# Fourier attention on one core: ScalarE's rounding moved between cosine and sine, and the query projections, output projection, residuals and norms moved to other places within the chunks

## The reference

```python
def _fourier_kernel(x, proj_mat):
    p = jnp.einsum('blhd,dm->blhm', x, proj_mat) / math.sqrt(D_HEAD)
    return jnp.concatenate([jnp.cos(p), jnp.sin(p)], axis=-1) / math.sqrt(D_KMAP)
...
x2 = _layer_norm(x, ln1_g, ln1_b)
q = (x2 @ wq + bq).reshape(B, L, N_HEAD, D_HEAD)
k = (x2 @ wk + bk).reshape(B, L, N_HEAD, D_HEAD)
v = (x2 @ wv + bv).reshape(B, L, N_HEAD, D_HEAD)
qp = _fourier_kernel(q, proj_mat)
kp = _fourier_kernel(k, proj_mat)
kv = jnp.einsum('blhm,blhd->bhmd', kp, v)
attn = jnp.einsum('blhm,bhmd->blhd', qp, kv)
attn = attn.reshape(B, L, D_MODEL) @ wo + bo
x = x + attn
```

## Time and profile before

| | us |
|---|---|
| device time, three runs | 891.72, 892.42, 892.43 (median 892.42) |
| device time of the profiled execution | 885.71 |
| its span, first to last instruction | 883.9 |
| busy in the span: PE, DVE, ACT, POOL | 731.3, 686.8, 570.6, 394.5 |
| mean granted TensorE clock | 0.903 of full speed |
| K0 to Q3, from the first cosine of K0 to the copy of the last output | 225.4 |

### The profile page before, as it was taken

How to read it: one execution, slowest core, us unless ns; L and a number is a source line. 1 busy time by engine, 2 the same in 40 slices (tenths; PEclk the granted TensorE clock), 3 DMA queues, 4 the chain that set the end, 5 groups by cost and what they waited for, 6 DMA issues and landing times. The chain is left out here.

```text
span 883.9 us, 11015 instructions
## 1 busy us (share of the span) xinstructions
PE 731.3 (83%) x3306; PEld 469.4 (53%) x3306; DVE 686.8 (78%) x1615; ACT 570.6 (65%) x926; POOL 394.5 (45%) x427
## 2 busy tenths in 40 slices
PE   4788998779998889999778988877778767877787
PEld 3666765445555567777566867643223222222565
DVE  6685786798998638777767888968899778786785
ACT  5264664657474435664636767667899879777776
POOL 6638665634345105555329977534323332230330
PEclk9999998988697669999969999987899889789999
DMA  4200000100000000000001000000000000000001
GB/s 134 72 12 13 16 16 18 34 24 25 13 25 19 0 1 1 1 1 0 1 0 37 1 1 0 1 0 1 1 0 1 1 1 0 1 0 1 1 1 48
DMA packets 9610, 11.59 MB, mean 13 GB/s; under 512 B 720, under 2 KB 5712, under 8 KB 9552
## 3 DMA queue, kind: packets, MB, share of 16 engines
q1 hardware_dynamic: 9552, 10.89, 4.3%
HBM read 9.84 MB, written 1.05 MB: 12 GB/s over the span
## 5 line engine op out<-in xcount | busy, mean ns | idle before, releaser
L1032 POOL TENSOR_TENSOR rbuf<-B,rbuf 128x512 fp32r<-128x512 f32 x96 | 124.1, 1295 | 83.6 <-ACT rbuf L960 83.4
L497 POOL TENSOR_SCALAR small<-small 128x4 f32<-128x4 f32 x32 | 8.5, 265 | 173.3 <-DVE small L387 172.8
L994 DVE TENSOR_TENSOR B<-B,up_banks 128x512 f32<-128x512 f32 x68 | 46.4, 683 | 42.3 <-PE up_banks L733 25.8
L945 ACT ACTIVATE B<-gate_banks 128x512 f32<-128x512 f32 x68 | 40.6, 599 | 59.4 <-PE gate_banks L733 58.3
L960 ACT ACTIVATE rbuf<-B 128x512 fp32r<-128x512 f32 x100 | 62.5, 625 | 17.3 <-DVE B L1010 12.3
L1010 DVE TENSOR_TENSOR B<-B,spread_bank 128x512 f32<-128x512 f32 x96 | 64.7, 678 | 11.0 <-ACT B L949 7.0
L1757 ACT ACTIVATE B<-B,VEC 128x1024 f32<-128x1024 f32 x48 | 55.3, 1151 | 22.4 <-DVE B L1752 22.3
L731 PE MATMUL gate_banks<-XH,WH 128*128 128x512 f32 x152 | 67.0, 441 | 0.8 <-ACT YT L1355 0.8
L733 PE MATMUL gate_banks<-XH,WL 128*128 128x512 f32 x152 | 62.4, 410 | 0.0
L732 PE MATMUL gate_banks<-XL,WH 128*128 128x512 f32 x152 | 62.3, 410 | 0.0
L949 ACT ACTIVATE B<-gate_banks,WR 128x512 f32<-128x512 f32 x64 | 44.0, 689 | 27.3 <-PE gate_banks L733 26.7
(11 more groups left out here) (347 smaller groups left out, 2274.3 us busy)
## 6 DMA issues: line engine op xcount, KB each, us to landing
STG<-in_w_split SPq DMA_DIRECT2D x27, 256.0 KB, 2.7
X<-in_x SPq DMA_DIRECT2D x4, 256.0 KB, 5.0
out<-X SPq DMA_DIRECT2D x4, 256.0 KB, 2.3
WR<-in_w_raw SPq DMA_DIRECT2D x1, 524.5 KB, 4.4
STG<-in_w_exact SPq DMA_DIRECT2D x2, 256.0 KB, 2.6
STG<-in_w_split SPq DMA_DIRECT2D x5, 64.0 KB, 1.9
STG<-in_w_split SPq DMA_DIRECT2D x1, 192.0 KB, 2.4
STG<-in_w_split SPq DMA_DIRECT2D x1, 128.0 KB, 2.0
```

What stands on the lines that cost most here:

```text
L994: nc.vector.tensor_tensor(MO[n % 2], AO[n % 2], U[n % 2][:, :], ALU.mult).then_inc(mul_done, 1)
L1032: e_.tensor_tensor(lo, hidden(f, n), hi.bitcast(F32), ALU.subtract).then_inc(hl_ready, 1)
```

## The change

In both halves of the stage ScalarE's order within a slot becomes cosine of p, projection copy, round of p+2, sine of p; it was cosine, sine, round, (output or YT copy,) projection copy. The rounds of pairs 19 and 27 (slot 3 of K2 and K3) go from ScalarE to VectorE. The projections of Q1 to Q3 begin two slots earlier (TensorE in slots 0 to 3, copies and splits in 1 to 4). The split of the attention output goes from VectorE (slot 2) to GpSimd (slot 1, ahead of the first projection split); the product with wo goes from slot 1 to slot 4 and waits for the last projection copy, its copy YT from slot 2 to slot 5. In the query bodies the tail goes on TensorE from slot 3 (1 in Q0) to 5 and on VectorE from slot 4 (2 in Q0) to 7; norm steps go to slots 1, 3 and 6 on VectorE, 2 and 3 on GpSimd, 4 on TensorE and 5 on ScalarE. KVT is filled in slot 2 of Q0 and not in slot 1. In FFN2's table two steps trade places by two blocks (2 from 7 to 9, 8 from 9 to 8, 9 from 11 to 10, 3 from 8 to 11).

```diff
-            16: {..., 5: (6,), 7: (2, 7), 8: (3,), 9: (8,), 11: (9,), 14: (10,)},
+            16: {..., 5: (6,), 7: (7,), 8: (8,), 9: (2,), 10: (9,), 11: (3,), 14: (10,)},
...
-            if cp > NC + 1 and s_ == 0:
-                pe.wait_ge(yt_ready, count(6, cp - NC - 2) + 1)
+            if cp > NC + 2 and s_ == 0:
+                pe.wait_ge(yt_ready, count(6, cp - NC - 3) + 1)
...
         def rounds_on_act(p):
-            return p % 2 == 1
+            return p % 2 == 1 and not (p // UP in (2, 3) and p % UP == 3)
...
-            s_ = n - (1 if cp <= NC else 2)
+            s_ = n - (1 if cp <= NC else 0)
...
         def lin_pool(g, cp, hook):
             for n in range(UP):
+                if n == 1 and cp > NC:
+                    project_pool(g, cp - NC - 1)
                 if lin_projects(cp + 1, n - 1) is not None:
                     lin_split(nc.gpsimd, g, cp + 1, lin_projects(cp + 1, n - 1))
-                lin_hooks(n, hook, 1, {0: (0,), 1: (1,)})
+                lin_hooks(n, hook, 1, {0: (0,), 1: (1,)} if cp < NC else {2: (0,), 3: (1,)})
...
         lin_pe
-                if n == 1 and cp > NC:
+                if n == 4 and cp > NC:
                     project_pe(pe, cp - NC - 1)
-                lin_hooks(n, hook, 1 if cp in (0, NC) else 3, {2: (2,)})
+                if cp < NC:
+                    lin_hooks(n, hook, 1 if cp == 0 else 3, {2: (2,)})
+                else:
+                    lin_hooks(n, hook, 5, {4: (2,)})
...
         lin_act
-                lin_trig(a, p)
-                if rounds_on_act(p):
+                lin_cos(a, p)
+                if lin_projects(cp + 1, n - 1) is not None:
+                    lin_proj_act(a, cp + 1, lin_projects(cp + 1, n - 1))
+                if rounds_on_act(p + 2):
                     lin_round_act(a, p + 2)
+                lin_sin(a, p)
...
-                if n == 2 and cp > NC:
+                if n == 5 and cp > NC:
                     project_act(a, cp - NC - 1)
-                lin_hooks(n, hook, 3, {3: (2,)})
+                lin_hooks(n, hook, 3, {3: (2,)} if cp < NC else {5: (2,)})
...
         lin_dve
-                if n == 2 and cp > NC:
-                    project_dve(v, cp - NC - 1)
-                if cp == NC and n == 1:
+                if cp == NC and n == 2:
...
-                lin_hooks(n, hook, 2 if cp in (0, NC) else 4, {0: (0,), 1: (1,), 2: (11,), 4: (3,)})
+                if cp < NC:
+                    lin_hooks(n, hook, 2 if cp == 0 else 4, {0: (0,), 1: (1,), 2: (11,), 4: (3,)})
+                else:
+                    lin_hooks(n, hook, 7, {1: (0,), 3: (1,), 6: (3,)})
...
         def project_pe(pe, c):
-            pe.wait_ge(al_ready, NC + c + 1)
+            pe.wait_ge(proj_sb, proj_no(min(NC + 2 + c, 2 * NC - 1), 3) + 1)
+            pe.wait_ge(ol_ready, c + 1)
...
+        def project_pool(g, c):
+            g.wait_ge(oq_read, c + 1)
             if c:
-                v.wait_ge(y_full, count_y(6, c))
+                g.wait_ge(y_full, count_y(6, c))
+            nc.gpsimd.tensor_scalar(rbuf[0][:, :], A32[:, :], 1.0, 0.0, ALU.mult, ALU.add).then_inc(oh_ready, 1)
+            g.wait_ge(oh_ready, c + 1)
+            nc.gpsimd.tensor_tensor(rbuf[1][:, :], A32[:, :], rbuf[0][:, :].bitcast(F32), ALU.subtract)\
+                .then_inc(ol_ready, 1)
```

## The result

The changed kernel takes 878.09 us (median of four executions, 876.92 to 880.40); the kernel before, on the same chip, 892.31 (four, 891.72 to 892.43). The ratio is 0.9845 with a 95% interval of 0.9824 to 0.9867. Timed again later beside the kernel before (888.17), the unchanged new kernel took 878.17: 0.9874 (0.9839 to 0.9908). So the gain is 14.2 us between the medians of the one comparison and 10.0 between those of the other; the forecast was 8.5, and a time of 883.9.

The account below looks back on a forecast made before the run. ScalarE was taken to bound K2, with VectorE's work as large and waits between them lengthening the other stretches. Terms for K0 to Q3 and the ring summed to -8.5: 892.42 to 883.9 us, range 877 to 890.5 (own range 879 to 888).

Parts of the forecast that it names:

- the ring: After Q3: the last output split on GpSimd slows VectorE's first subtraction beside it; +0.6 us (0 to 1.0).
- full gain: Rival, chance 0.15: ScalarE keeps its backlog, no odd copy waits, K0 to K2 lose nothing; 4.4 more, 879.5 us.
- FFN2's table: FFN2: norm turn and split later, two routing steps one block earlier, hidden by the blocks' matmuls; 0, within -1 and +1.
- the wait of the copies: Odd slots: 14 projection copies ahead of the round wait for TensorE; 9.3 us in the sum, K0 +2.9, K1 +0.9.
- The XH step: K0, slot 3: X32 and XH come 1.8 us later, the XL subtraction gives 0.95 back; net +0.85.
- the moved rounds: K2, K3: 1.0 off ScalarE, 1.22 more for VectorE; with waits at sign and copies, K2 +0.6, K3 -1.3.
- the boundary: Ends of Q0 to Q2: TensorE's slot 6 stall for the fourth projection split goes, at most 3.4 each; K3's by 1.3.
- KVT in Q0: Slots 1 and 2 of Q0: products and first projection wait for KVT, ScalarE idles 2.9; Q0 26.2 us (-3.1).
- Q2: Query body with a norm: VectorE idles 3.4 for GpSimd's late deviation, XH waits 2.0 for X32; 30.0 us (-1.5).
- Q3: Last query body, no projections, deviation in time: VectorE's work plus 1.3 waiting for X32; 25.0 us (-1.8).
- POOL as a new wait: Rival, chance 0.12: late deviation and splits, signs slowed beside GpSimd, Q1 27 and Q2 31.5; -3.3, 889.1 us.
- copies ahead of rounds: Rival of a slower kernel, chance 0.08: the 14 odd copies wait 1.6 each; +4.6, 897.0 us.

Follow-up runs that it names:

- e3: New kernel with only the projection copy moved behind the sine on ScalarE (cosine, round, sine, copy): 875.70 us, 0.9888 of the kernel before.
- e4: New kernel with ScalarE's old order (cosine, sine, round, copy) in both halves: 873.09 us, 0.9848 of the kernel before.
- e7: New kernel with the rounds of pairs 19 and 27 kept on ScalarE: 876.49 us, 0.9877 of the kernel before.
- e5: New kernel with KVT filled in slot 1 of Q0 again, as before: 878.92 us, 0.9886 of the kernel before.
- e8: New kernel with the copy behind the sine and GpSimd's first norm step ahead of the second projection split: 874.43 us, 0.9854 of the kernel before.
- e10: New kernel with ScalarE's old order, both rounds kept on ScalarE, KVT in slot 1 and GpSimd's norm step first: 868.62 us, 0.9759 of the kernel before.
- e2: New kernel with FFN2's old table: 886.35 us, 0.9985 of the kernel before.
- e6: New kernel with GpSimd's first norm step of the query bodies ahead of its second projection split: 878.27 us, 0.9876 of the kernel before.
- e9: New kernel unchanged, run again as a yardstick: 878.17 us, 0.9874 of the kernel before.
- e12: As e10, but with the attention output's split back on VectorE in slot 2: 869.43 us, 0.9785 of the kernel before.
- e1: Kernel before with only FFN2's new table: 882.42 us, 0.9937 of the kernel before.
- e11: Kernel before with only the norm's turn and split later in FFN2's table, routing steps at their old blocks: 879.90 us, 0.9899.

## Why the prediction came out, step by step

The time fell into the range by luck. By profiles, the sum was right because 7.1 us that I had not seen ahead of the stage stood in for 5.9 that the stage and 1.0 that the ring fell short. The measured 878.09 is just below the forecast's own 879 to 888, nearest to the full gain's 879.5, whose mechanism is not what happened.

**Failed: FFN2's table, "the blocks' matmuls hide them: 0".** It measured -7.1. The trace of before had the answer and I didn't look: TensorE's waits grouped over FFN2 name X and SC for 14.3 us in six waits. I took the matmuls behind a moved step as its cover. But a step that waits holds up TensorE's queue, and the matmuls behind it are what is held up. The sentence "no row shows the table in another order" hid that the rows show what the old order cost.

**Held in number, half in mechanism: the wait of the copies.** K0 and K1 cost 3.6 against 3.8, and the wait that I forecast is in the rows: copies wait 3.78 in K0 and 3.65 in K1, 0.25 and 0.21 before. The XH step was 4.32 of waiting, 2.4 more than the earlier trace rows (1.8 forecast), and the XL subtraction did fall from 1.66 to 0.69. But the cost isn't the copy's: with the copy behind the sine (e3) K0 and K1 stay at 64.6, and only with the round behind it too (e4) do they fall, to 60.2. I counted the round ahead of the sine as a gain of 0.94 for VectorE; it comes before the products that free its buffer and waits for them. In Q1 the copy is the cause, and in Q0 in good part.

**Failed in sign: the moved rounds.** I counted 1.0 off ScalarE and 0.5 plus 1.15 of new waits, with the copies' order as the cause, and left the rounds as a gain within it. e7 shows 1.2 each lost by the move under the new order. The loop was level there: ScalarE had 0.7 less work in K3 than in e7, and waits of 0.59, 0.45 and 0.86 where e7 has none. K3's own gain, -0.7, hides that it could have been -1.9 (e7).

**Held: the boundary.** TensorE's waits for GpSimd's projection splits over the whole stage (total, times, longest), before and then new:

```profile
PE up_banks L1685 <- POOL WL L1663: 6.5, 2, 3.3
PE up_banks L1685 <- POOL WH L1663: 6.4, 2, 3.3
PE up_banks L1682 <- POOL WH L1663: 1.8, 2, 1.1
PE up_banks L1682 <- POOL WL L1663: 1.1, 1, 1.1
```

```profile
PE up_banks L1684 <- POOL WH L1665: 2.9, 1, 2.9
```

The four waits of some 3.2 in slot 6 (the earlier trace rows has two) are gone, also the one at K3's end, of which only 1.3 was forecast to go. The one left is in K0, at 596.27; the same instruction waited 2.56 before, for VectorE's rest, so it isn't new. Q1 is 24.16 for a forecast 23.3 (e3 and e4, without the copy's wait, 23.4 and 23.5).

**Mis-sized: KVT in Q0.** 2.9 forecast, 3.92 measured at the copy: Q0 27.19, not 26.2. The runs show two waits in one: 0.8 is KVT's slot (e5), and 1.9 the copy's place ahead of the round (3.92 to 1.99 in e8, 3.16 to 1.20 from e5 to e10).

**Mis-sized: Q2.** Forecast 30.0, measured 32.06. The wait for the deviation was right (3.4 forecast, 3.94 measured). Left out: the normalising that follows runs beside GpSimd's next split and takes 2.35, not 1.1, and ScalarE idled 4.54, not 3.3. XH waited 2.82 for X32, not 2.0. In the profile of before the same operation took 4.34 in FFN2, so the row was there.

**Q3.** 25.0 forecast. The runs show two levels of it, 24.79 to 24.86 (e2, e4, e6, e7, e10) and 26.00 to 26.20 (new, e9, e3, e5, e8), with no edit that divides them. The granted clock divides them: 1.00 in the first five, 0.93 in the others, and in these a round waits 1.1 to 1.3 for TensorE's products that waits for nothing in the first. (e12, at 0.93, has 25.73.) The step was right for the first level, and what picks the level stays open.

**The ring: +0.6, measured +1.6.** Two parts. The split beside the first subtraction costs what was summed, and 0.67 in the row itself, not "about a microsecond" as in the prediction's text. VectorE in the new kernel, where it took 0.69 before:

```profile
807.94 1.36 DVE L2038 TENSOR_TENSOR WE<-B,SCT 128x512 fp32r<-128x512 f32 x1 [4.53 <-ACT SCT L2012]
```

From the output copy to the norm's turn on TensorE it is 7.32 us now, 6.66 before and 6.66 in e12 (split on VectorE): +0.66. By the Trainium skill (GPSIMD Engine Reference, 1. Specifications) VectorE instructions with two SBUF inputs contend with GpSimd, and this row agrees: 1.36 for 0.69. The other 0.95 is TensorE's clock. ScalarE's copy behind its matmuls starts 2.78 after the norm's turn, 1.83 before. The turn of YT, which comes right behind the norm's, and the first gate matmuls after it, before and then new:

```profile
823.57 0.60 PE L749 MATMUL norm_bank<-WR,YT 128*128 128x128 f32 x4
823.92 0.48 PE L731 MATMUL gate_banks<-XH,WH 128*128 128x512 f32 x1
824.24 0.39 PE L732 MATMUL gate_banks<-XL,WH 128*128 128x512 f32 x1
```

```profile
813.91 0.96 PE L751 MATMUL norm_bank<-WR,YT 128*128 128x128 f32 x4
814.53 0.77 PE L733 MATMUL gate_banks<-XH,WH 128*128 128x512 f32 x1
815.11 0.63 PE L734 MATMUL gate_banks<-XL,WH 128*128 128x512 f32 x1
```

TensorE had waited about as long ahead of the norm's turn (2.91 now, 3.04 before). All three kernels with the old queries (before, e1, e11) stay at the full level there, and all eleven profiles with the new ones fall to the lower. It isn't the split on GpSimd: e12 has it on VectorE and falls too. Which other edit of the queries decides it was not tried and stays open.

**From the profile to the median.** I added 6.7 us for the gap between the profiled execution of before and its median. It didn't carry over: the new kernel's median is 1.2 above its profiled execution. This alone puts the forecast time 5.5 of its 5.8 us too high.

**The rivals.** None is the case. The one of POOL as a new wait is true in Q2 alone. That of the slower kernel, copies ahead of rounds, has part of its mechanism: the whole order costs 7.8 in the stage (the difference to e4, 1.3 of it in Q3's two levels, in K0 and K1 by the round's place) where the forecast held 9.3 for copies. It did not decide, but it used up most of what the boundary gave: without the table the new kernel stands at 0.9985.

## What to carry to other kernels

Look at the waits of every stage that a change touches, grouped by releaser, before an edit is priced at nothing: a table line that shifts a step by two blocks was worth more than all the work on the stage (7.1 and 3.2 us). A step that can wait belongs in the queue where its input is ready, however much work stands around it, because what stands behind it waits too. In a loop between two engines at equal load, edits don't add up (a round earlier wins 2.0, a round moved 0.7, both lose 0.5 in K2 and K3), so run them apart. And before an edit is blamed for a stretch, see how far kernels with the same code in it differ.

## What the runs showed of the hardware

VectorE's normalising (128 partitions by 128 elements, four times, one SBUF tensor and scalars from SBUF) took 1.12 us by itself (812.25, GpSimd idle), and 2.35, 2.81 and 4.34 where GpSimd worked beside it for 1.9, 2.6 and 4.2 us (new at 759.98, e6 at 763.25, before at 557.92). So it lost 1.2, 1.7 and 3.2 us, each time less than that work lasted. The subtractions of two SBUF tensors lost 0.97 and 0.67 (1.66 and 1.36 for 0.69), with 1.1 and 0.8 of GpSimd's work beside them. So both forms lost between six and nine tenths of the time that they shared with GpSimd's work, and such a step is to be priced by the GpSimd work beside it.

The second finding is that the clock of a whole stretch can differ between kernels that have the same code in it (Q1 0.87 and 1.00, 27.26 and 24.16 us), while two executions of one kernel agreed within 0.10 in every stretch. A lower clock and a longer stretch go together in K2 (0.93 and 1.00, 24.58 and 23.26), Q0 (0.93 and 1.00, 26.56 and 25.23, e3 and e8) and Q3 as well, each time with a longer wait of ScalarE for TensorE's products or projection. What sets it in one kernel and not in another was not found.
